# Cross attention for eight batches on one core: the visit moves to step 2 of a slot, its sums over keys go right behind it, and the first fills of unit 1 go to GpSimd

## The reference

```python
q = (queries @ Wq.T + bq).reshape(B, Nq, HEADS, D_K).transpose(0, 2, 1, 3)
k = (keys @ Wk.T + bk).reshape(B, Nk, HEADS, D_K).transpose(0, 2, 1, 3)
v = (values @ Wv.T + bv).reshape(B, Nk, HEADS, D_K).transpose(0, 2, 1, 3)
att = jnp.einsum('bhqd,bhkd->bhqk', q, k) / np.sqrt(D_K).astype(np.float32)
att = jax.nn.softmax(att, axis=-1)
out = jnp.einsum('bhqk,bhkd->bhqd', att, v)
out = out.transpose(0, 2, 1, 3).reshape(B, Nq, HEADS * D_K)
out = out @ Wo.T + bo
out = queries + out
mean = jnp.mean(out, axis=-1, keepdims=True)
var = jnp.var(out, axis=-1, keepdims=True)
out = (out - mean) / jnp.sqrt(var + 1e-05) * gamma + beta
```

## Time and profile before

| | |
|---|---|
| median of 3 runs | 644.46 us (643.81 to 645.33) |
| profiled execution, its own time | 644.03 us |
| span of the profiled execution | 642.0 us |
| PE busy | 617.8 us (96%) |
| DVE busy | 480.1 us (75%) |
| POOL busy | 453.5 us (71%) |
| ACT busy | 350.5 us (55%) |
| chain that ended last | PE 81%, DVE 15%, issue 2% |

### The profile page before, as it was taken

How to read it: one execution, slowest core, us unless ns; L and a number is a source line. 1 busy time by engine, 2 the same in 40 slices (tenths; PEclk the granted TensorE clock), 3 DMA queues, 4 the chain that set the end, 5 groups by cost and what they waited for, 6 DMA issues and landing times.

```text
span 642.0 us, 13640 instructions
## 1 busy us (share of the span) xinstructions
PE 617.8 (96%) x5217; PEld 422.1 (66%) x5217; DVE 480.1 (75%) x680; ACT 350.5 (55%) x673; POOL 453.5 (71%) x443
## 2 busy tenths in 40 slices
PE   9989999999999999999999999999999999999994
PEld 7756676766666667766666666666677666665542
DVE  4677677777887688776887678876888788765895
ACT  4524566565565456564665655654565656443661
POOL 9401686975878588785879858785887878866853
PEclk9999999999999999999999999999999999999998
DMA  9367633663256613754137631566136431330011
GB/s 298 127 180 166 148 85 73 125 149 67 63 112 140 147 42 89 162 138 107 28 87 162 146 77 47 128 148 143 35 89 165 99 66 40 96 91 21 2 50 37
DMA packets 96016, 67.02 MB, mean 104 GB/s; under 512 B 69892, under 2 KB 82192, under 8 KB 95952
## 3 DMA queue, kind: packets, MB, share of 16 engines
q1 hardware_dynamic: 95952, 66.16, 41.9%
HBM read 24.52 MB, written 3.67 MB: 44 GB/s over the span
## 4 chain that ended last, share of the span: by engine, by line
PE 81%; DVE 15%; issue 2%; ACT 1%; POOL 0%; POOLq 0%; DVEq 0%
PE ps_task L595 36%; PE ps_task L646 11%; PE ps_scores L606 11%; PE ps_scoresT L630 10%; DVE top L912 6%; PE ps_task L554 4%; PE ps_task L672 2%; PE ps_scores L595 2%; DVE attn_sums L919 2%; DVE attn_parts L934 2%; DVE y L881 1%; DVE stats L884 1%; DVE parts L869 1%; PE ps_scores L574 1%; PE ps_scores L658 1%
## 5 line engine op out<-in xcount | busy, mean ns | idle before, releaser
L793 ACT ACTIVATE probsT<-ps_scoresT 125x448 f32<-125x448 f32 x384 | 203.8, 545 | 200.6 <-PE ps_scoresT L630 198.9
L912 DVE TENSOR_REDUCE top<-ps_scores 112x1 f32<-112x750 f32 x256 | 235.4, 927 | 78.8 <-PE ps_scores L606 77.8
L1020 POOL TENSOR_TENSOR pair_sums<-probsT 125x672 f32<-125x672 f32 x122 | 198.5, 1627 | 111.0 <-ACT probsT L793 101.8
L630 PE MATMUL ps_scoresT<-stacks 100*125 100x224 f16 x768 | 134.8, 260 | 1.7 <-ACT probsT L793 1.1
L595 PE MATMUL ps_task<-wvT,ctxT 128*125 128x512 f16 x564 | 134.9, 379 | 0.9 <-DVE parts L869 0.9
L595 PE MATMUL ps_task<-ctxT,wkT 128*128 128x375 f16 x708 | 130.7, 323 | 0.1
L606 PE MATMUL ps_scores<-stacks 96*112 96x512 f16 (+1 forms) x512 | 126.2, 328 | 2.5 <-DVE top L912 2.5
L630 PEld LDWEIGHTS ps_scoresT<-stacks 100*125 100x125 f16 x768 | 93.6, 137 | 40.9 <-ACT probsT L793 6.4
L1025 POOL TENSOR_TENSOR head_sums<-pair_sums 125x224 f32<-125x224 f32 x122 | 88.8, 728 | 11.4
L595 PEld LDWEIGHTS ps_task<-wvT,ctxT 128*125 128x125 f16 x564 | 73.2, 136 | 33.7 <-DVE parts L869 1.1
L1028 POOL TENSOR_TENSOR head_sums<-head_sums,pair_sums 125x224 f32<-125x224 f32 x122 | 87.1, 714 | 9.6
(11 more groups left out here) (100 smaller groups left out, 524.1 us busy)
## 6 DMA issues: line engine op xcount, KB each, us to landing
stacks<-parts SPq DMA_DIRECT2D x256, 60.9 KB, 2.0
ctx_in<-in_ctx SPq DMA_DIRECT2D x8, 768.0 KB, 5.6
stacks<-parts SPq DMA_DIRECT2D x128, 46.9 KB, 2.0
resid<-in_x SPq DMA_DIRECT2D x8, 448.0 KB, 4.2
ctx_in<-in_ctx SPq DMA_DIRECT2D x7, 512.0 KB
out_y<-y SPq DMA_DIRECT2D x16, 224.0 KB, 2.4
x_in<-in_x SPq DMA_DIRECT2D x8, 256.0 KB, 3.1
stacks<-parts SPq DMA_DIRECT2D x128, 14.0 KB, 1.8
```

Of the source, the lines that this page charges most:

```text
L630: last = nc.tensor.matmul(ps_scoresT[0:KP, piece % 2, NQ * i:NQ * i + NQ], stacks[:, g, h, KP * k:KP * k + KP], stacks[:, g, h, Qc], start ...
L793: nc.scalar.activation(probsT[0:KP, g % 2, h, 2 * j:2 * j + 2, :].rearrange("p k q -> p (k q)"), ps_scoresT[0:KP, piece % 2, 0:2 * NQ], AC ...
L912: nc.vector.tensor_reduce(top[0:QP, g % 2, HG * q + h:HG * q + h + 1], ps_scores[0:QP, s % RING, 0:NK], AX.X, ALU.max).then_inc(top_ready, 1)
L1020: nc.gpsimd.tensor_tensor(pair_sums[0:KP], probsT[0:KP, g % 2, h, 0:3, :], probsT[0:KP, g % 2, h, 3:6, :], ALU.add).then_inc(pair_sums_rea ...
```

## The change

It has four parts.

1. `VISIT` goes from 1 to 2. The visit now stands in step 2 of a slot, with `sum_keys` directly behind it. The tasks of step 2 go to step 1: Q2 from 2 to 1, V5 from 10 to 9, Q1 from 26 to 25, and the first half of the output projection from 18 to 17. Two of the three pieces of step 2 go to step 1, inside and behind its task. Where ScalarE and VectorE split incoming tokens moves too (`SPLIT`).
2. V2 of the first batch and three of the four transposes of Wo leave the prologue. They become tasks of the first iteration in steps 2, 10, 17 and 20 (`FIRST`). Wo is loaded in two halves, the second of them into `y`, after the biases that lay there have been read.
3. GpSimd issues the 16 DMAs that fill unit 1's stacks for the first batch. SyncE loads the next batch's context before it fills unit 0.
4. `EVEN` starts at step 16 of the last batch and not at step 8.

```diff
-    PIECES_IN = ((0, 0, 0), (0, 0, 0), (1, 1, 1), (1, 0, 0), (1, 1, 0), (1, 1, 1), (1, 0, 0), (1, 1, 0)) * UNITS
+    PIECES_IN = ((0, 0, 0), (0, 1, 1), (1, 0, 0), (1, 0, 0), (1, 1, 0), (1, 1, 1), (1, 0, 0), (1, 1, 0)) * UNITS
...
+    WO_HALF = DT // 2
...
-    VISIT = 1
-    OWN = {0: ("K", 2, 1), 2: ("Q", 2), 4: ("K", 3, 1), 5: ("V", 3), 7: ("V", 4), 8: ("Q", 3), 10: ("V", 5)}
+    VISIT = 2
+    OWN = {0: ("K", 2, 1), 1: ("Q", 2), 4: ("K", 3, 1), 5: ("V", 3), 7: ("V", 4), 8: ("Q", 3), 9: ("V", 5)}
...
-            26: ("Q", 1), 28: ("V", 2), 29: ("K", 2, 0), 31: ("K", 3, 0)}
-    SPLIT = {1: (("ctxT", 0), ("ctxT", 1)), 2: (("ctxT", 2),), 9: (("ctxT", 3), ("ctxT", 4)), 10: (("ctxT", 5),),
-             17: (("xT", 0), ("xT", 1))}
+            25: ("Q", 1), 28: ("V", 2), 29: ("K", 2, 0), 31: ("K", 3, 0)}
+    SPLIT = {1: (("ctxT", 0),), 2: (("ctxT", 1), ("ctxT", 2)), 10: (("ctxT", 3), ("ctxT", 4), ("ctxT", 5)),
+             18: (("xT", 0), ("xT", 1))}
...
-    OUTPUT = {18: ("O", 0), 20: ("O", 1)}
+    OUTPUT = {17: ("O", 0), 20: ("O", 1)}
+    FIRST = {2: ("V", 2), 10: ("W", "o", 1), 17: ("W", "o", 2), 20: ("W", "o", 3)}
...
-    SUMS_BEHIND = 2
-    STAGES = {**{("attend", k): (2, VISIT) for k in range(KT)}, "sum_keys": (2, SUMS_BEHIND), "copy": (2, 3), ("invert", 0): (2, 4),
+    STAGES = {**{("attend", k): (2, VISIT) for k in range(KT)}, "sum_keys": (2, VISIT), "copy": (2, 3), ("invert", 0): (2, 4),
...
-        found.update(OUTPUT if not known or b > 0 else {})
+        found.update(OUTPUT if not known or b > 0 else FIRST)
...
+        wo_in = (w_in[:, 3, 0:WO_HALF], y[:])
...
+        stacked_by_pool = [sem(f"stacked_by_pool{h}") for h in range(HG)]
...
-            table = EVEN if isinstance(b, int) and (b == B or b == LAST and s >= UNIT) else PIECES_IN
+            table = EVEN if isinstance(b, int) and (b == B or b == LAST and s >= 2 * UNIT) else PIECES_IN
...
+        def fill_stack(eng, g, filled):
+
+            for h in range(HG):
+                rows_of_h = slice(DK * h, DK * h + DK)
+                for r, (q_part, k_part) in enumerate(SPLIT_ROWS):
+                    to = slice(DK * r, DK * r + DK)
+                    if q_part != k_part:
+                        eng.dma_start(stacks[to, g, h, :], parts[rows_of_h, g, k_part, :]).then_inc(filled[h], DMA)
+                    else:
+                        eng.dma_start(stacks[to, g, h, Kc], parts[rows_of_h, g, k_part, Kc]).then_inc(filled[h], DMA)
+                        eng.dma_start(stacks[to, g, h, Qc], parts[rows_of_h, g, 1 - q_part, Qc]).then_inc(filled[h], DMA)
...
-            load_w("o", Wo)
+            load_wo_half(0)
+            sp.wait_ge(bias_turned, 1)
+            load_wo_half(1)
             sp.wait_ge(task_saved, prologue.index(("Q", 0)) + 1)
-            fill_stack(0)
             load_ctx(1, 0)
+            fill_stack(sp, 0, stacked[0])
             load_x(1)
...
-            sp.wait_ge(task_saved, prologue.index(("Q", 1)) + 1)
-            fill_stack(1)
             load_resid(0)
...
-                    sp.wait_ge(task_ready, after(LAST_READERS[t]) if t in LAST_READERS else before)
+                    sp.wait_ge(task_ready, after(LAST_READERS[t]) if t in LAST_READERS else before + moved_readers)
...
-                    pe.wait_ge(stacked[g][h], DMA * STACK_DMAS * (batch + 1))
+                    if g != 1:
+                        pe.wait_ge(stacked[g][h], DMA * STACK_DMAS * (batch + 1))
+                    elif isinstance(batch, int) and batch == 0:
+                        pe.wait_ge(stacked_by_pool[h], DMA * STACK_DMAS)
+                    else:
+                        pe.wait_ge(stacked[g][h], DMA * STACK_DMAS * batch)
...
-                    if s % UNIT != SUMS_BEHIND:
-                        for u, g_u in due("sum_keys", b, s):
-                            sum_keys(u, g_u)
+                    for u, g_u in due("sum_keys", b, s):
+                        sum_keys(u, g_u)
...
-                    if s % UNIT == SUMS_BEHIND:
-                        for u, g_u in due("sum_keys", b, s):
-                            sum_keys(u, g_u)
...
+            pool.wait_ge(task_saved, prologue.index(("Q", 1)) + 1)
+            fill_stack(pool, 1, stacked_by_pool)
             pool.wait_ge(rows_loaded, 3 * DMA)
```

More of the change, by code:

```diff
@@ L104, in build @@
     SPLIT_KINDS = ("ctxT", "xT", "K", "Q", "W")
-    prologue = [("W", "k", 0)] + [("ctxT", i) for i in range(3)] + [("xT", 0), ("xT", 1), ("W", "k", 1), ("W", "k", 2), ("K", 0, 0),
[4 rows of a table removed]
+    prologue = [("W", "k", 0), ("ctxT", 0), ("ctxT", 1), ("ctxT", 2), ("xT", 0), ("xT", 1), ("W", "k", 1), ("W", "k", 2),
[3 rows of a table added]
     PRO = len(prologue)
@@ L477, in after @@
                     return before + max(tasks[STEP_OF[t]][1] for t in kinds) + 1
+                moved_readers = max((place + 1 for s, (t, place, _) in tasks.items() if isinstance(b, int) and b == 0 and s in FIRST and t[0] == "V"), default=0)
                 def wait_split(t):
@@ L570, in task @@
                 elif kind == "W":
-                    if t[1] == "k" or t[2] == 0:
+                    if t[1] == "o":
+                        pe.wait_ge(wo_loaded[t[2] // WO_HALF], DMA)
+                    elif t[1] == "k" or t[2] == 0:
                         pe.wait_ge(w_loaded[t[1]][t[2]], DMA)
+                    for piece in inside:
+                        scores_keymajor(*piece)
+                    rows_in = wo_in[t[2] // WO_HALF][:, t[2] % WO_HALF] if t[1] == "o" else w_in[:, "qkv".index(t[1]), t[2]]
                     for k in range(DT):
-                        last = nc.tensor.transpose(bank[:, P * k:P * k + P], w_in[:, "qkvo".index(t[1]), t[2], P * k:P * k + P], ident[:])
+                        last = nc.tensor.transpose(bank[:, P * k:P * k + P], rows_in[:, P * k:P * k + P], ident[:])
                 elif kind == "O":
```

27 lines of the change are left out of this document (11 added, 16 removed), and 7 rows, old and new, of the table prologue.

## The result

The changed kernel takes 638.96 us (median of four runs, 637.98 to 640.04), the kernel before on the same chip 644.34: a ratio of 0.9911, 95% interval 0.9899 to 0.9922. It is faster by 5.4 us; 12.9 were forecast, and 638.96 lies outside the range of 627.5 to 637. The span of the profiled execution fell from 642.0 to 637.3 us. The table goes from the first scores of one stretch to the first of the next, read from the timeline of TensorE. The forecasts are before's times with the prediction's terms put where they act: in iteration 0 the moved work adds 0.57 (2.97 less the net 2.4) and two sums over keys take 0.52 away; in iteration 6 the terms take 1.44, in iteration 7 0.66, 0.26 and 1.3.

A forecast was written before the change was run, and what follows sets the result against it. TensorE, busy 96% of the span, bounds the kernel through its list and gaps. The terms 7.2 + 2.8 + 2.4 + 1.3 - 0.8 = 12.9 us, off 644.03, give 631.0 us; 8-in-10 range 627.5 to 637.

The forecast's parts named there:

- The sums behind the visit: Sums over keys directly behind the visit cost 0.40 instead of 0.66: 0.26 saved 28 times, 7.2 us, bounds 5.9 to 8.5.
- The wait behind VectorE: TensorE's waits for VectorE's save, step 25 of iterations 1 to 6 and in iteration 7, shrink: 2.8 us of 6.0.
- Both would shift alike, so I leave it at 1.47: VectorE's low part of the attention and GpSimd's addition beside it move together, so the low part stays at 1.47 us.
- A new closeness: Sums over keys come soon after GpSimd's last addition, 0.3 to 1 us in hand; 0.8 us set aside for waits.
- the first rival: The sums over keys wait for GpSimd in unit 3's slot, 0.7 to 1 us in six or seven slots: 637; chance 0.11.
- Prologue and first iteration: First scores start 2.97 us earlier; the 3.9 us of moved work fills iteration 0's idle time: net gain 2.4 us.
- GpSimd's fills: GpSimd's 16 DMAs for unit 1, started at 27.45, delay no work on TensorE: no cost.
- x = 2.08: Time in us each of the 16 DMAs must hold GpSimd before TensorE waits at the first sums over keys.
- SyncE was waited for by no one: Ridding SyncE of 16 fills gains nothing, since no engine waited for it.
- The end: In iteration 7 the output half fills TensorE's 0.79 gap ahead of scores, plus 0.5 for the maximum: 1.3 us.
- only hands the gain on: Behind that place in iteration 7 VectorE is the bound and passes the gain on unchanged.
- nothing that lowers it: TensorE's clock was granted in full in the profile's rows, and nothing was seen to lower it.

The follow-up runs named there:

- experiments 7: The kernel of experiment 1 with the sums over keys taken from behind the visit into step 3, behind that step's scores and piece: 640.71 us.
- experiment 1: The changed kernel with GpSimd's `rstd` of the first output half moved from step 19 to step 20, behind head 0's addition: 633.45 us.
- experiment 6: The kernel of experiment 1 with the second output half's `rstd` also one addition later, in step 23 behind head 2's: 628.88 us.
- experiment 4: The changed kernel with V2 and Wo's tiles 1 to 3 back in the prologue, as in the kernel before: 640.43 us.
- experiment 2: The changed kernel with context token splits 3 and 4 back in step 9, only split 5 left in step 10: 643.59 us.
- experiment 3: The changed kernel with unit 1's first 16 row copies issued on SyncE's queue, none on GpSimd: 638.13 us.
- experiment 9: The fastest kernel: that of experiment 6 with token splits 3 and 4 in step 9 and GpSimd's output bias additions in step 12: 626.70 us.
- experiment 10: The kernel of experiment 9 with unit 1's first 16 row copies on SyncE's queue, none on GpSimd: 631.40 us.

## Why the prediction was wrong

**The sums behind the visit: right.** 7.2 us forecast, 7.3 by the medians and 6.5 by the traces between experiments 7 and 1. The price of the sums there, 0.40 forecast, is 0.39. (The term's upper bound does not follow from its text: 0.1 more for each of 28 visits is 10.1, not 8.5. Nothing rests on it.)

**The wait behind VectorE: right in size only once GpSimd's order is mended.** In experiment 1, where GpSimd keeps its time, 0.46 is left in step 25 of iterations 1 to 6, and 0.42 was forecast; in iteration 7 1.05 is left of 1.11, where 0.7 was forecast. In the changed kernel itself the wait in step 25 is gone altogether: GpSimd, late by the next point, stood at its second `rstd` and not at an addition when the low part came at 381.33, which took 0.44. The step "Both would shift alike, so I leave it at 1.47" failed: they did not shift alike. The Trainium skill ("SBUF — State Buffer", section "SBUF: two separate sides") has VectorE and GpSimd share a port pair as an exclusive lock, the loser waiting for the whole instruction. The rows agree that one of the two stands still: the low part takes 1.47 us beside an addition of 1.61, the two `token_low` 3.72 beside 2.51 + 1.63, and when GpSimd loses, its 0.66 becomes 1.33. Who loses can't be told from the start times in the rows: GpSimd's instruction began first in experiment 1 and in experiment 6, and VectorE's was the longer in the one, GpSimd's in the other.

**A new closeness: the failing step.** The text had the cause, `rstd` ahead of head 0's sum, and then a wrong end of the chain: GpSimd at 391.0 to 391.7 on before's clock, where 0.3 to 1 us were left. It missed by 1.2 to 1.9 us: the second `rstd` was itself long (1.56 for 0.55), GpSimd never caught up, and the sums waited 0.89 in six iterations, 5.3 us where 0.8 were set aside (start to start each costs 1.1). This was the first rival's mechanism, at a chance of 0.11. Undoing it alone gives 5.5 us back by the medians (experiment 1), and GpSimd's last addition of the unit then ends 1.8 us earlier against the start of its iteration.

**Prologue and first iteration: the second failing step.** The prologue gave 3.03 (2.97 forecast); that it fits so closely is in part luck, since the first scores of experiments with this same prologue began anywhere from 35.32 to 36.23. The moved work takes 1.7 us in iteration 0 (experiment 4) where the sum of 2.4 left 0.6 for it, so the part is worth 1.0 to 1.5 us net. The 2.4 rested on the idle time of the first iteration being free for it, and another edit made a new gap there: all three splits of that slot now stand in step 10, and GpSimd's first addition (57.88) has begun when they do (58.34), while before two of them were done in step 9 ahead of it. That is 1.4 us (experiment 2). I had counted nothing for the splits.

**GpSimd's fills: right for this kernel.** 0.50 us an issue, done at 36.1, long before x = 2.08 would have mattered; and SyncE's relief shows no gain here that can be told from none (experiment 3). This does not carry over: in the fastest kernel the relief is worth 4.7 us (experiment 10). The kernel before has its splits as early and its copies on SyncE, issues that load at 50.30, and nothing waits for it, but its first scores begin 2.6 us later than experiment 10's. So "SyncE was waited for by no one" holds for one arrangement only.

**The end.** Slot 2 of iteration 7 gained 1.41 (1.3 forecast). Slot 1 gained 0.83, of which the sums explain 0.26; no run separates the rest, for which nothing was counted. The last stretch lost 0.5, against "only hands the gain on", and experiment 1 takes that back. Slot 0 lost 2.25 instead of gaining. There two VectorE instructions with both operands in SBUF were stretched: L915 took 2.10 and L950 2.16, against 1.15 and 1.42 before. Q2 waited 1.85, and the granted clock fell behind the wait, where the prediction had seen "nothing that lowers it". With GpSimd's order mended the slot is 18.75 (experiments 1, 6, 9). Why the clock fell in this profile and not in experiment 3's, behind an equal wait, stays open. It seems to change from one execution to the next: of the changed kernel's four runs two have a mean granted clock of 0.994 and spans of 637.3 and 637.6 us, two have 0.996 and 636.2 and 636.7.

**The account.** By the traces the span fell by 4.7 us where 12.9 were forecast. The 8.2 us between them are about 2.8 in iteration 0, 3.5 in iterations 1 to 6, 2.7 in iteration 7 and 0.1 behind the last scores, less the 0.8 that had been set aside. Experiment 1 gives 6.2 us back, all in iterations 1 to 7 (1.6 of it is the clock): an iteration is then the forecast 73.5, and iteration 7 is 0.4 shorter than forecast. Iteration 0's 2.8 stay: 1.1 because the moved work takes 1.7 and not 0.6, 1.4 for the splits, and the rest small.
